# Attention on one Trainium2 core: bank pairs of row and transposed scores swapped, and their mask products moved in TensorE's order

## The reference, cut to what matters

```
qkv    = n.reshape(b_, n_, H, HD).transpose(0, 2, 1, 3)      # H 8, HD 16
scores = einsum('bhqd,bhkd->bhqk', qkv, qkv) / sqrt(HD)
masked = where(adj > 0, scores, -inf)
attn   = softmax(masked, axis=-1)
out    = einsum('bhqk,bhkd->bhqd', attn, qkv)
x      = x + out                                             # then an MLP
```

## Time and profile before

| what | us |
|---|---|
| median of 3 runs | 2773.0 (2771.43 to 2773.26) |
| the profiled execution, its own time | 2770.89 |
| its span, first to last instruction | 2769.0 |
| TensorE matmul busy, of the span | 2675.4 (97%) |
| VectorE / ScalarE / GpSimd busy | 1938.7 / 1461.0 / 1506.1 |

### The profile page before, as it was taken

One profiled execution on the slowest core, in us unless ns is written; L12 is line 12 of the kernel. 1 busy time (PEld: TensorE's weight loads), 2 busy tenths in 40 slices (PEclk: granted clock), 3 DMA queues, 4 the chain that ended last, 5 costly groups with the idle time before them and its releaser, 6 DMA issues. The chain is left out here.

```text
span 2769.0 us, 85746 instructions
## 1 busy us (share of the span) xinstructions
PE 2675.4 (97%) x28783; PEld 2143.5 (77%) x28784; DVE 1938.7 (70%) x6630; ACT 1461.0 (53%) x2930; POOL 1506.1 (54%) x2542
## 2 busy tenths in 40 slices
PE   8999999899979999999999899998998999999999
PEld 4666666599967888888878677777778999999888
DVE  6777777477778888888888577777864455544453
ACT  3555445455546666666666454444554444444444
POOL 5555555233335555555555447776752666666664
PEclk9999999999999999999999999999999999999999
DMA  1111111000000000000000011111422222222264
GB/s 53 35 34 34 34 31 47 2 0 0 0 2 0 0 0 0 0 0 0 0 0 0 21 41 58 58 54 54 129 72 67 78 77 76 77 78 81 70 202 143
DMA packets 158117, 118.26 MB, mean 43 GB/s; under 512 B 20150, under 2 KB 145593, under 8 KB 158010
## 3 DMA queue, kind: packets, MB, share of 16 engines
q1 hardware_dynamic: 140602, 81.02, 10.5%
q0 software_dynamic: 17408, 35.95, 3.8%
HBM read 68.36 MB, written 48.56 MB: 42 GB/s over the span
## 5 line engine op out<-in xcount | busy, mean ns | idle before, releaser
L2027 POOL DMA_INDIRECT token_y<-e_y,e_rows x288 | 295.2, 1025 | 78.8 <-issue 72.1
L2070 ACT ACTIVATE e_hidden<-e_ps,e_b1g 128x512 f32<-128x512 f32 x288 | 194.6, 688 | 258.3 <-PE e_ps L90 257.7
L1303 POOL DMA_INDIRECT sorted_z<-r_z,r_rows x256 | 263.8, 1031 | 67.2 <-issue 62.8
L842 POOL TENSOR_TENSOR s_sw<-s_expo,s_rsum 128x512 f32<-128x512 f32 x128 | 133.6, 1044 | 297.3 <-DVE s_rsum L1100 297.3
L2122 PE MATMUL e_ps<-expert_w,e_hidden 128*128 x2304 | 280.3, 275 | 0.0
L2122 PEld LDWEIGHTS e_ps<-expert_w,e_hidden 128*128 128x128 f32 x2304 | 273.9, 192 | 6.3
L514 DVE TENSOR_REDUCE a_V<-a_ps_s 128x8 f32<-128x1024 f32 x128 | 156.9, 1226 | 129.6 <-PE a_ps_s L394 129.6
L2199 DVE TENSOR_TENSOR e_biased<-e_ps,expert_b 128x512 f32<-128x512 f32 x72 | 49.8, 691 | 213.9 <-PE e_ps L2122 213.9
L394 PE MATMUL a_ps_s<-a_nT 16*128 16x128 f32 x2048 | 184.9, 298 | 0.1
L402 PE MATMUL a_ps_st<-a_topT,a_nT 17*128 17x128 f32 x2048 | 183.6, 297 | 0.1
L394 PEld LDWEIGHTS a_ps_s<-a_nT 16*128 16x128 f32 x2048 | 135.6, 187 | 45.5 <-issue 45.2
(11 more groups left out here) (400 smaller groups left out, 8094.8 us busy)
## 6 DMA issues: line engine op xcount, KB each, us to landing
e_z<-sorted_z SPq DMA_DIRECT2D x72, 260.0 KB
c_y<-token_y SPq DMA_DIRECT2D x22, 512.0 KB, 4.1
X<-in_x_dram SPq DMA_DIRECT2D x32, 256.0 KB, 2.8
a_adj<-in_adj_dram SPq DMA_DIRECT2D x32, 256.0 KB, 2.8
g_adj<-in_adj_dram SPq DMA_DIRECT2D x32, 256.0 KB, 2.9
out_dram<-X SPq DMA_DIRECT2D x32, 256.0 KB, 2.5
c_y_s<-token_y SPq DMA_DIRECT2D x10, 512.0 KB, 4.9
token_y<-e_y,e_rows POOLq DMA_INDIRECT x288
```

The source lines that it names most:

```text
L842: nc.gpsimd.tensor_tensor(sw[p][:, :, :], expo[p][:, :, :], rsum[p][:, 1, :].unsqueeze(2).to_broadcast([T, HEADS, C]), ALU.mult).then_inc( ...
L1303: nc.gpsimd.indirect_dma_start(sh.sorted_z, bass.IndirectOffsetOnAxis(ap=rows[own][:, e * GB + piece:e * GB + piece + 1], axis=0), zr[own] ...
L2027: nc.gpsimd.indirect_dma_start(sh.token_y, bass.IndirectOffsetOnAxis(ap=rows[p][:, b:b + 1], axis=0), y[p][:, b, :], None).then_inc(y_scat ...
L2070: nc.scalar.activation(hidden[p][:, c, :], ps_1[c % 2][:, :], ACT.Gelu, bias=b1g[p][:, c:c + 1]).then_inc(s["hidden_done"], 1)
```

## The change

Row scores get two bank pairs, taken by b % 2, and transposed scores one. On TensorE the row scores' mask product moves up to just behind the turn of the input, without the waits for `nT_done` and `top_done`; the `nT_done` wait now stands just ahead of the score products, and `top_done` is left only between the two halves, where it stood already. The transposed scores' mask product moves down, behind the result's turn, and waits for `prob_done` of graph k-3 in place of k-4, since the one bank pair must have been read by the exponential of the graph before.

```diff
-        ps_s, ps_st = ps("a_ps_s", [T, 2, 4, T]), [ps(f"a_ps_st{i}", [T, 2, 4, T]) for i in range(2)]
+        ps_s, ps_st = [ps(f"a_ps_s{i}", [T, 2, 4, T]) for i in range(2)], ps("a_ps_st", [T, 2, 4, T])
...
-                        nc.scalar.activation(probT[b % 2][:, :, :, :], ps_st[b % 2][:, :, :, :], ACT.Exp,
+                        nc.scalar.activation(probT[b % 2][:, :, :, :], ps_st[:, :, :, :], ACT.Exp,
...
-                    nc.tensor.matmul(ps_st[0][:, i % 2, :, :], sh.ident_bf[:, :],
+                    nc.tensor.matmul(ps_st[:, i % 2, :, :], sh.ident_bf[:, :],
...
                         last.then_inc(s["n_turned"], 1)
-                    if live(kk, 2, n_graphs):
-                        own, i = (p, b - 2) if b >= 2 else (q, b + 2)
-                        if since(kk, 4):
-                            pe.wait_ge(s["prob_done"], k - 3)
-                        for c in range(2):
-                            nc.tensor.matmul(ps_st[b % 2][:, c, :, :], edge_bias[own][:, i, :],
-                                             sh.ident_bf[:, :].unsqueeze(1).to_broadcast([T, 4, T]),
-                                             start=True, stop=False)
                     if live(kk, 0, n_graphs):
                         if b == 0:
                             pe.wait_ge(s["bias_done"], t - 1)
-                        pe.wait_ge(s["nT_done"], k + 1)
-                        if since(kk, 1):
-                            pe.wait_ge(s["top_done"], k)
                         for c in range(2):
-                            nc.tensor.matmul(ps_s[:, c, :, :], sh.ident_bf[:, :],
+                            nc.tensor.matmul(ps_s[b % 2][:, c, :, :], sh.ident_bf[:, :],
                                              edge_bias[p][:, b:b + 1, :].to_broadcast([T, 4, T]),
                                              start=True, stop=False)
                     if live(kk, 4, n_graphs):
...
                         last.then_inc(s["o_turned"], 1)
                     if live(kk, 2, n_graphs):
+                        own, i = (p, b - 2) if b >= 2 else (q, b + 2)
+                        if since(kk, 3):
+                            pe.wait_ge(s["prob_done"], k - 2)
+                        for c in range(2):
+                            nc.tensor.matmul(ps_st[:, c, :, :], edge_bias[own][:, i, :],
+                                             sh.ident_bf[:, :].unsqueeze(1).to_broadcast([T, 4, T]),
+                                             start=True, stop=False)
+                    if live(kk, 0, n_graphs):
+                        pe.wait_ge(s["nT_done"], k + 1)
+                    if live(kk, 2, n_graphs):
                         pe.wait_ge(s["topT_done"], k - 1)
...
```

More of the change, by code:

```diff
@@ L393, in step @@
                                     side = nT[p][32 * tile:32 * tile + HD, b, c, :]
-                                    last = nc.tensor.matmul(ps_s[:, j, 2 * half + c, :], side, side, start=False,
+                                    last = nc.tensor.matmul(ps_s[b % 2][:, j, 2 * half + c, :], side, side, start=False,
                                                             stop=(half == 1 and c == 1))
@@ L401, in step @@
                                     rows = slice(32 * tile, 32 * tile + HD + 1)
-                                    last = nc.tensor.matmul(ps_st[b % 2][:, j, 2 * (1 - half) + c, :], nT[own][rows, i, c, :],
+                                    last = nc.tensor.matmul(ps_st[:, j, 2 * (1 - half) + c, :], nT[own][rows, i, c, :],
                                                             topT[(b + 2) % 4][rows, c, :], start=False,
@@ L514, in step @@
                         nc.vector.reduce_max(V[p][:, b, :, TOP].rearrange("p (c i j) -> p j i c", c=2, j=2),
-                                             ps_s[:, :, :, :].rearrange("p j (i c) n -> p j i c n", c=2), AX.X).then_inc(s["top_done"], 1)
+                                             ps_s[b % 2][:, :, :, :].rearrange("p j (i c) n -> p j i c n", c=2), AX.X).then_inc(s["top_done"], 1)
             run_steps(dve, step, groups, LAG, PEEL)
```

## The result

The changed kernel takes 2789.8 us (median of 4 runs, 2788.1 to 2792.5), the one before 2773.1 beside it: 1.0058 times as long, with an interval of 1.004 to 1.0075. That is slower by some 16.7 us, where 12.5 were forecast and 2785.5 named. Direction, mechanism and range (2773 to 2794) held; the size was a quarter too small. The profiled execution took 2788.06 us, its span is 2786.3.

What follows compares the result with a forecast made beforehand. A loop through VectorE's maximum (3.90 us a turn) was taken as the bound, then ScalarE's exponential-to-oT loop (4.00): 12.4 us over 124 turns, +0.9 and -0.8 at the ends, 12.5 on 2773.0 is 2785.5 us; range 2773 to 2794.

Steps and rivals of the forecast that it cites:

- Two loops, and only one wait removed: Attention turn: VectorE's maximum loop (3.90 us) loses its wait; ScalarE's exponential-to-oT loop remains and sets 4.00 us.
- The transposed mask product paid in full: On TensorE between oT and the scores: moved behind the result's turn, it makes turn to scores 0.80 us.
- The lower and upper bounds: Limits for result's turn to first score product: 0.71 us and 0.89 us, around the 0.80 taken.
- the hidden step: Rival: the tile-width change hides under the mask product's tail, 0.71 for 0.80, +1.2 us, 2774; chance 0.11.
- the dear restart: Rival: TensorE's stalled restart at the result's turn costs more, 0.89 us, period 4.09, +23.6 us, 2797; chance 0.09.
- The added wait for the exponential is met by oT: Transposed mask product's new wait costs nothing, since ScalarE runs oT behind that exponential; turn to mask product 0.28 us.
- Slack elsewhere: No wait at the maxima's turn; division keeps 0.46 us before the values' product; VectorE idle about 1.24 us.
- The period as the same for all turns: Graphs 4 to 127: each of 124 turns takes 0.10 us more, 12.4 us together.
- The ends: Attention phase's edges: graph 1's dropped wait gives about -0.8 us, two turns after the last row scores add 0.9.
- TensorE as the bound, 3.70 us a turn, 2748: Rival: TensorE's own work sets the attention turn if oT comes 0.24 us earlier, -25 us; chance 0.07.

Runs made afterwards that it cites:

- The experiments with one additional matmul: Changed kernel plus one more 512-column matmul a turn: ahead of the row mask product 2793.2 us, behind the result's turn 2816.0 us.
- the bank pairs alone: Kernel before with the changed kernel's bank pairs, its order of mask products and result's turn kept: 2804.1 us, 1.0086 times before.
- the turn between the halves: Changed kernel with both mask products in a row, row scores first, and result's turn between the score products' halves: 2754.6 us, 0.9919 times before.

## Why the prediction was right, and where its size was off

*Two loops, and only one wait removed.* Right. The period is the forecast 4.00 in three turns of four, and the steps of its sum measured 1.30, 0.05, 0.80 and 1.85 as they stood there. The experiments with one additional matmul show the same from outside. The two releases of the earlier trace rows lie 0.04 us apart (202.59 for the row mask product, 202.58 + 0.05 = 202.63 for the result's turn), not the 0.01 that I wrote; no term of the sum uses it.

*The transposed mask product paid in full.* Right; 0.80 from turn to scores, not 0.71 or 0.89. The lower and upper bounds are out, and so are the rivals of the hidden step and the dear restart.

*The added wait for the exponential is met by oT.* Right: turn to mask product is 0.27 or 0.28 us, without a wait.

*Slack elsewhere.* Right in kind: nothing waits at the turn of the maxima, and the division ends 0.57 us ahead of the product with the values in the turn with the most norm work, 0.46 before. VectorE's idleness ahead of the maximum is 1.40 to 1.46 us in three turns of four, where it had been at most 1.15, not the 1.24 I named. The result's turn now stands 0.80 us ahead of the scores in place of 0.31, so VectorE no longer waits for it (8.8 us in total from 100 to 500 us before, none shown now), and its idleness gathers ahead of the maximum.

*The period as the same for all turns* is the term that was mis-sized. I took 124 x 0.10 = 12.4 us. Measured from the fifth exponential on, 121 distances take 487.9 us, 93 of 4.00 and 28 of 4.15, where the same 121 took 471.6 before: 16.2 us. The 0.15 belong to ScalarE's and TensorE's register instructions behind a release, 0.08 each. ScalarE's half was to be seen before: the distance from the values' product to the exponential, 0.16 us in the earlier trace rows, is 0.24 in every fourth turn of the kernel before, and the exponentials there come at 3.90, 3.90, 3.98 and 3.82. The mean stays 3.90 because that loop was not the one that set it. TensorE's half was hidden behind the row mask product. I read one turn of four and carried its distances to all.

*The ends.* Graph 1's wait went, and gave 1.06 us: the 0.80 that I took is the idle time shown behind a modelled end, and by the distances between starts (22.57 to 24.05 us before, 22.90 to 23.38 after) the mask product alone came 1.00 us closer. At the other end, 17.1 us lie between the two kernels from the fifth exponential to the last oT (499.09 against 481.98 us), which leaves 0.9 beyond the 16.2, as forecast. The start as a whole cost 2.7 us in the profile instead of giving 0.8, through the later clock; I had left a microsecond for that.

The sum in the profiled executions: 2.7 + 17.1 = 19.8 us at the end of attention (551.04 against 531.24), and the phases behind it, which the change does not touch, took 2235.3 against 2237.8 us, 2.5 less. 19.8 - 2.5 = 17.3, the difference of the spans. Those 2.5 us are not the change's: over all thirteen profiles these phases took from 2235.3 to 2251.1 us. That the 2.7 of the start and these 2.5, neither of them forecast, nearly cancel is luck.

*TensorE as the bound, 3.70 us a turn, 2748* was my rival for the other sign. It fell for this change, since oT comes 0.24 us too late for it. But its numbers are those of the best version: 3.70 a turn and 2749.1 us, reached by leaving the transposed mask product ahead of the turn, where it covers the wait for oT. The rule that I cited there from the Trainium skill ("Perfetto Trace Analysis", section "Matmuls"), to rotate independent groups through different banks so that evacuation overlaps the next group, agrees with the best version (3.90 to 3.70 us a turn) and not with this change or with the bank pairs alone (4.11): the rotation pays where the order leaves work to cover the wait that remains.

## What to carry to other kernels

When two waits end within a few hundredths of a microsecond, removing one gives the distance to the next and no more; write down both loops before the change, and treat every instruction that moves behind the remaining release as an addition of its full length. Work that is free of the wait belongs ahead of it: the same two mask products made a turn 4.00 or 3.70 us by standing behind or ahead of one pair of transposes. Read as many turns as the code's unrolling has variants, since a loop that is hidden now can have a slow turn that shows only once it sets the pace.

## What the runs showed of the hardware that was not expected

Where the wait stood on a register instruction ahead of the real one, ScalarE and TensorE each started 0.07 to 0.08 us later behind the release; with constants in its place the delay is gone (4.15, 4.07, 4.00 us a turn).

TensorE's clock can stay at 0.50 (1.2 GHz) for a long time under a dense stream. In the profile with the turn between the halves the busy time by stretch gives TensorE as busy throughout, and still at half clock:

```profile
40.00:50.00 10.00, 10.00 (x85) 5.85 (x83) 3.05 (x12) 2.11 (x4) 2.35 (x5) 0.50 0.10 28
...
70.00:80.00 10.00, 10.00 (x95) 6.18 (x95) 5.44 (x16) 4.15 (x8) 4.71 (x11) 0.50 0.01 2
```

A turn took 6.7 us there in place of 3.70, and that execution 2783.6 us where the kernel's median is 2754.6. The moment of the rise differs between executions of one kernel by more than 20 us (from about 43 to the stretch from 60 to 70 us in the changed one), and with it the time by more than the effects of some of these experiments. The clock costs time elsewhere as well: at the phase's end, where several profiles have it back at 0.50 before the last turn (the last distance 5.27 and 5.38 us in place of 3.70), and in the phases behind, where one execution lost 15.8 us on another of the same kernel with a mean of 0.83 against 0.95 from 1700 to 1800 us.
